# A transformer block on one core: the products of weights and values from f16 halves in three passes

## What is computed

```python
qkv = jnp.einsum('bsh,oh->bso', x, w_qkv)
q, k, v = jnp.split(qkv, [H * D, (H + HKV) * D], axis=-1)
...
scores = jnp.einsum('bhqd,bhkd->bhqk', q, k) / jnp.sqrt(jnp.float32(D))
causal = jnp.triu(jnp.ones((s, s), dtype=bool), k=1)
scores = jnp.where(causal, -jnp.inf, scores)
weights = jax.nn.softmax(scores, axis=-1)
attn = jnp.einsum('bhqk,bhkd->bhqd', weights, v)
attn = attn.transpose(0, 2, 1, 3).reshape(b, s, H * D)
return jnp.einsum('bsd,od->bso', attn, w_o)
```

## Time and profile before

| | us |
|---|---|
| median of 3 runs | 1461.82 |
| lowest and highest | 1461.27, 1463.99 |
| the profiled execution, its own time | 1461.52 |
| its span | 1459.7 |
| TensorE busy | 1370.3 (94%) |
| VectorE busy | 861.9 (59%) |
| ScalarE busy | 649.9 (45%) |
| GpSimd busy | 393.5 (27%) |

### The profile page before, as it was taken

How to read it: one execution, slowest core, us unless ns; L and a number is a source line. 1 busy time by engine, 2 the same in 40 slices (tenths; PEclk the granted TensorE clock), 3 DMA queues, 4 the chain that set the end, 5 groups by cost and what they waited for, 6 DMA issues and landing times.

```text
span 1459.7 us, 31431 instructions
## 1 busy us (share of the span) xinstructions
PE 1370.3 (94%) x11264; PEld 876.5 (60%) x11264; DVE 861.9 (59%) x2052; ACT 649.9 (45%) x1447; POOL 393.5 (27%) x311
## 2 busy tenths in 40 slices
PE   2699999999999999799999999999999679999997
PEld 1466666666666666556666666666666445555554
DVE  8877777777777777734454444545445587444433
ACT  2433333333333333436666666666666312232322
POOL 6644444444444444211112111111211283000000
PEclk9799999999999999899999999999999899999999
DMA  8300000000000000311111112111111440000000
GB/s 276 118 1 0 0 0 0 0 0 0 0 0 0 0 0 0 128 59 49 43 42 42 42 42 70 56 42 42 42 42 30 196 145 1 24 1 22 0 24 23
DMA packets 22271, 58.34 MB, mean 40 GB/s; under 512 B 1262, under 2 KB 9454, under 8 KB 19026
## 3 DMA queue, kind: packets, MB, share of 16 engines
q1 hardware_dynamic: 22226, 57.74, 12.0%
HBM read 54.46 MB, written 3.28 MB: 40 GB/s over the span
## 4 chain that ended last, share of the span: by engine, by line
PE 88%; DVE 6%; POOL 2%; issue 2%; ACT 1%; DMA 1%; DVEq 0%; SPq 0%; POOLq 0%; ACTq 0%
PE A L1386 20%; PE A L1302 16%; PE A L1354 11%; PE C L1607 10%; PE C L1410 6%; PE B L1427 5%; PE C L1340 3%; PE C L1321 3%; PE A L1622 3%; PE B L1622 3%; PE B L1395 2%; PE B L1313 2%; PE B L1333 1%; PE B L1434 1%; POOL qk L476 1%
## 5 line engine op out<-in xcount | busy, mean ns | idle before, releaser
L1302 PE MATMUL A<-arena,xh 128*100 128x512 f16 x768 | 184.1, 383 | 22.6 <-DVE arena L1054 14.4
L1386 PE MATMUL A<-wxh,arena 128*122 128x512 f16 x768 | 198.4, 381 | 0.0
L1607 PE MATMUL C<-arena 128*128 128x400 f16 x1024 | 188.4, 338 | 8.7 <-DVE arena L982 8.7
L424 POOL TENSOR_TENSOR arena<-arena,region 100x512 f32<-100x512 f32 (+1 forms) x64 | 65.9, 1062 | 427.0 <-DVE region L943 427.0
L401 POOL TENSOR_TENSOR region<-tb,ub 100x512 f32<-100x512 f32 x80 | 108.5, 1356 | 265.1 <-DVE ub L830 265.1
L1354 PE MATMUL A<-arena,stageb 128*100 128x512 f16 x768 | 175.8, 379 | 0.7 <-ACT arena L569 0.7
L1607 PEld LDWEIGHTS C<-arena 128*128 128x128 bf16 x1024 | 101.8, 99 | 85.5 <-issue 15.4
L1302 PEld LDWEIGHTS A<-arena,xh 128*100 128x100 f16 x768 | 94.7, 126 | 93.1 <-issue 20.9
L522 ACT ACTIVATE region<-C,negm 100x100 f32<-100x100 f32 x256 | 84.2, 347 | 145.9 <-DVE negm L869 145.9
L585 ACT ACTIVATE arena<-C 122x1600 f32<-122x1600 f32 x96 | 144.4, 1504 | 4.6 <-PE C L1410 2.5
L1354 PEld LDWEIGHTS A<-arena,stageb 128*100 128x100 f16 x768 | 94.0, 125 | 62.7 <-ACT arena L569 1.1
(11 more groups left out here) (174 smaller groups left out, 2318.3 us busy)
## 6 DMA issues: line engine op xcount, KB each, us to landing
stageb<-in_wffn SPq DMA_DIRECT2D x16, 768.0 KB, 4.7
arena<-in_ctxt SPq DMA_DIRECT2D x16, 722.0 KB, 4.6
stageb<-in_wffn SPq DMA_DIRECT2D x8, 1024.0 KB, 4.8
arena<-in_wqkv SPq DMA_DIRECT2D x4, 1024.0 KB, 13.8
arena<-in_wffn SPq DMA_DIRECT2D x4, 1024.0 KB, 5.8
out_x<-xres SPq DMA_DIRECT2D x16, 200.0 KB
arena<-in_wx SPq DMA_DIRECT2D x3, 1024.0 KB, 8.2
xres<-in_x SPq DMA_DIRECT2D x1, 3000.0 KB
```

Source lines behind the costliest of these rows:

```text
L424: pool.tensor_tensor(t, t, r, ALU.mult).then_inc(sig["g_kn"], 1)
L1302: ins = pe.matmul(A[j % 2][0:S, :], xp[:, k, :], wp[:, j, k, :], start=(n == 0), stop=(n == 11))
L1386: ins = pe.matmul(A[(par + n) % 2][0:rows, :], lhs, wp[:, 0 if n == 0 else 1 if n < 4 else 2, k, :], start=(i == 0), stop=(i == 11))
L1607: ins = pe.matmul(C[2 * (e % 2) + half][:, 0:UB * S], wf[:, 3 * (e // 4) + half, k, (e % 4) * 128:(e % 4 + 1) * 128], part[:, k, :], start ...
```

## The change

The turned weights and the values are each kept as two f16 halves (ph and pl, vh and vl, scaled by SP = 256 and SV = 32), and `attend` sums three f16 products, vh x ph, vh x pl and vl x ph, in place of one with fp32 operands. ScalarE makes the high halves in the copies that it made before. VectorE makes the low halves with five new instructions a batch: `p_lo` for each group, `v_lo` once. TensorE's waits for a_pT and a_v become waits for d_plo and d_vlo. The factor 1 / (SP SV) goes into a_hi and a_lo. Where one wait of TensorE implies another, the other is left out.

```diff
-        pT = carve([S, H * S])
+        ph = carve([S, H * S], F16)
+        pl = carve([S, H * S], F16)
...
-        vv = sb("vv", [S, HKV * D])
+        vh = sb("vh", [S, HKV * D], F16)
+        vl = sb("vl", [S, HKV * D], F16)
...
             def v_of(b):
...
-                act.activation(vv[:], A[1][0:S, :], ACT.Copy, scale=1.0 / (SX * SW)).then_inc(sig["a_v"], 1)
+                act.activation(vh[:], A[1][0:S, :], ACT.Copy, scale=SV / (SX * SW)).then_inc(sig["a_v"], 1)
...
             def p_back(b, g):
                 wait(act, "pe_pT", b, g + 1)
                 wait(act, "pe_av", b - 1, g + 1)
-                act.activation(pT[:, g * 400:(g + 1) * 400], B[g % 2][0:S, 0:400], ACT.Copy)\
+                act.activation(ph[:, g * 400:(g + 1) * 400], B[g % 2][0:S, 0:400], ACT.Copy, scale=SP)\
                    .then_inc(sig["a_pT"], 1)
...
+            def p_lo(b, g):
+                wait(dve, "a_pT", b, g + 1)
+                wait(dve, "pe_av", b - 1, g + 1)
+                dve.scalar_tensor_tensor(pl[:, g * 400:(g + 1) * 400], B[g % 2][0:S, 0:400], SP,
+                                         ph[:, g * 400:(g + 1) * 400], ALU.mult, ALU.subtract)\
+                   .then_inc(sig["d_plo"], 1)
+
+            def v_lo(b):
+                wait(dve, "a_v", b, 1)
+                wait(dve, "pe_av", b - 1, 4)
+                dve.scalar_tensor_tensor(vl[:], A[1][0:S, :], SV / (SX * SW), vh[:], ALU.mult, ALU.subtract)\
+                   .then_inc(sig["d_vlo"], 1)
...
             proj(0, 4)
             dve.wait_ge(ld_x, 16)
+            v_lo(0)
             row_stats(1, ssq[:, 20:21])
...
                 row_stats(0 if last else b + 2, ssq[:, 20:21])
+                p_lo(b, 0)
+                p_lo(b, 1)
                 proj(b + 1, 4)
+                p_lo(b, 2)
+                p_lo(b, 3)
                 a_lo(b, 0)
                 head_norm(b + 1)
...
                 for g in range(1, 4):
                     a_lo(b, g)
+                v_lo(b + 1)
                 for g in range(4):
                     z_back(b + 1, g)
...
             wait(dve, "pe_zT", b, 5)
+            for g in range(2):
+                p_lo(b, g)
 
             st.chain(dve.memset(xssq, 1.0))
             row_stats2(1)
-            for n in range(3):
+            square_sums(0, 0)
+            for g in range(2, 4):
+                p_lo(b, g)
+            for n in range(1, 3):
                 square_sums(0, n)
...
             def x_turn(b):
 
                 wait(pe, "d_xn", b, 1)
-                wait(pe, "a_v", b - 1, 1)
+                wait(pe, "d_vlo", b - 1, 1)
...
             def project(b, j):
                 if j == 0:
-                    wait(pe, "a_xhi", b, 1)
                     wait(pe, "d_xlo", b, 1)
                     wait(pe, "d_x1", b - 2, 1)
                 elif j >= 2:
-                    wait(pe, "a_sq", b, j - 1)
-                    wait(pe, "d_t", b, j - 1)
+
                     wait(pe, "d_u", b, j - 1)
...
             def z_turn(b, g):
                 wait(pe, "g_z", b, g + 1)
                 if g < 2:
-                    wait(pe, "a_pT", b - 1, 3 + g)
+                    wait(pe, "d_plo", b - 1, 3 + g)
...
             def p_turn(b, g):
...
                 elif g >= 2:
-                    wait(pe, "a_pT", b, g - 1)
+                    wait(pe, "d_plo", b, g - 1)
...
             def attend(b, g):
-                wait(pe, "a_pT", b, g + 1)
+                wait(pe, "d_plo", b, g + 1)
                 if g == 0:
-                    wait(pe, "a_v", b, 1)
-                pe.matmul(C[g][:, 0:400], vv[:, g * D:(g + 1) * D], pT[:, g * 400:(g + 1) * 400],
-                          start=True, stop=True).then_inc(sig["pe_av"], 1)
+                    wait(pe, "d_vlo", b, 1)
+                n = 0
+                for v, pt in ((vh, ph), (vh, pl), (vl, ph)):
+                    ins = pe.matmul(C[g][:, 0:400], v[:, g * D:(g + 1) * D], pt[:, g * 400:(g + 1) * 400],
+                                    start=(n == 0), stop=(n == 2))
+                    n += 1
+                ins.then_inc(sig["pe_av"], 1)
...
             def scores2(b, u):
-                t = (2 * u + 1) // NC
-                wait(pe, "a_T", b, t + 1)
-                wait(pe, "d_T", b, t + 1)
+                if u == 0:
+                    wait(pe, "a_T", b, 1)
+                    wait(pe, "d_T", b, 1)
```

More of the change, by code:

```diff
@@ L35 @@
 SH = 8.0
+SP = 256.0
+SV = 32.0
 VW = 2 * XD
@@ L255, in build @@
                    d_xn=1, d_zT=5, d_xlo=1, d_negm=4, d_t=5, d_u=5, d_ssq=5, d_rstd=1, d_rinv=4,
-                   d_alo=4, d_x1=1, g_w=5, g_z=5, g_p=4,
+                   d_alo=4, d_x1=1, d_plo=4, d_vlo=1, g_w=5, g_z=5, g_p=4,
                    pe_xT2=1, pe_proj=7, pe_T=4, pe_sc=6, pe_pv=4, pe_oT=2,
@@ L535, in a_hi @@
                 act.activation(ah[:, 4 * g:4 * g + 4, :], C[g][:, 0:400].rearrange("p (h s) -> p h s", h=4),
-                               ACT.Copy, scale=SA).then_inc(sig["a_ahi"], 1)
+                               ACT.Copy, scale=SA / (SP * SV)).then_inc(sig["a_ahi"], 1)
             def ctx_hi(b):
@@ L880, in a_lo @@
                 dve.scalar_tensor_tensor(al[:, 4 * g:4 * g + 4, :],
-                                         C[g][:, 0:400].rearrange("p (h s) -> p h s", h=4), SA,
+                                         C[g][:, 0:400].rearrange("p (h s) -> p h s", h=4), SA / (SP * SV),
                                          ah[:, 4 * g:4 * g + 4, :], ALU.mult, ALU.subtract)\
                    .then_inc(sig["d_alo"], 1)
+            def p_lo(b, g):
[9 more added lines that the diff above has]
+                   .then_inc(sig["d_vlo"], 1)
             def add_attn(b):
@@ L1366, in project2 @@
                 if n == 0:
-                    wait(pe, "a_x2", b, 1)
                     wait(pe, "d_x2", b, 1)
@@ L1370, in project2 @@
                 elif n == 1:
-                    wait(pe, "a_ctx", b, 1)
                     wait(pe, "d_ctx", b, 1)
@@ L1512, in _ @@
             project_out(b)
-            wait(pe, "a_pT", b, 4)
+            wait(pe, "d_plo", b, 4)
             turn_heads(0, 0, 0)
@@ L1568, in turn @@
                 if end < 1:
-                    wait(pe, "a_x2", b + 2, 1)
                     wait(pe, "d_x2", b + 2, 1)
@@ L1582, in turn @@
                 if end < 2:
-                    wait(pe, "a_T", b + 1, 1)
-                    wait(pe, "d_T", b + 1, 1)
                     turn_heads(b + 1, 1, odd)
```

## The result

The changed kernel takes 1490.92 us (median; 1490.14 to 1497.78) against 1462.36: ratio 1.0205, 95% interval 1.0173 to 1.0237. It is 2% slower, by 28.6 us; 34.1 were forecast, on the side and by the mechanism forecast. The profiled execution took 1490.14 us with a span of 1488.3, 28.6 more than before. The run of 1497.78 had a mean granted clock of 0.978 where the others had 0.980 to 0.982; what differed in it isn't known, since only the one execution has a trace.

What follows compares the result with a forecast made beforehand. TensorE was taken to bound the self attention (busy 529.57 of 530.90 us). Fifteen turns +29.9, last batch +2.3 and start +1.9 gave +34.1 on 1461.52: 1495.6 us, range 1484 to 1506.

Steps and rivals of the forecast that it cites:

- The first stall: In a middle self-attention turn, TensorE's first product of weights and values waits for p_lo(0): 1.77 us.
- steps 1 and 2: p_lo(0) runs 299.54 to 300.11; the first product follows 0.15 us after, at 300.26 instead of 298.49.
- The second stall: In a middle self-attention turn, TensorE's third product waits for p_lo(2): 1.13 us.
- step 5: Third product of a middle turn starts at 303.09, a stall of 1.13 us; the fourth at 303.60, done at 304.11.
- the gain of the passes: Four products on TensorE take 2.04 us with three f16 passes each instead of 2.94: 0.90 us a batch.
- The upper end: Range end of 1506 us: p_lo at 0.61 adds 7.5 us, two register instructions before each p_lo another 3.
- The end of the group follows p_lo(3) one for one: In each turn, the end of the four products is set by p_lo(3), VectorE's last low half.
- The last batch: Self attention's final batch, with another order on VectorE: third product stalls 2.5 us, products end 2.3 us later.
- The start: v_lo(0) in front of row_stats(1) waits for ScalarE's value copy and delays the path by 1.9 us.
- The waits left out: Dropping TensorE's implied waits gains nothing; other end 7.2 us, from the gaps before scores2 in the cross attention.
- All hidden: Rival, 4%: VectorE reaches p_lo(0) early enough, both stalls go and only the passes count: 1449 us.
- 7% to a case: Rival, 7%: new idle pieces of 1.8 and 1.1 us in self attention bring TensorE's clock down: 1536 us.

Runs made afterwards that it cites:

- row_stats late: The changed kernel with row_stats of the batch after next moved from before the first p_lo to behind the last one: 1498.76 us, ratio 1.0255.
- the passes alone: The changed kernel without low halves (no p_lo, no v_lo), all three passes taking the high halves, TensorE waiting for ScalarE's copies again: 1452.89 us, ratio 0.9947.
- cover alone: The changed kernel with only project(b+1, 5) split, eight passes before the first product and four before the third: 1474.0 us, ratio 1.0086.
- cover and order: The changed kernel with project(b+1, 5) split and a_lo(1), z_turn, x_turn and v_lo(0) also moved: 1450.51 us, ratio 0.9924.

## Why the prediction was right, point by point

- **The first stall** (steps 1 and 2: 1.77 us) measured 1.54 in 13 of the 15 turns. VectorE started p_lo(0) 1.25 us after the turn of tile 1 began, where proj(4) had started 1.40 after it, and TensorE followed within 0.06 us and not 0.15.
- **The second stall** (step 5: 1.13) measured 1.10, **the gain of the passes** (0.90) 0.86: 2.94 less 4 x 0.52. Sum: 1.54 + 1.10 - 0.86 = 1.78 against 1.75 from the starts. The turn was forecast at +1.99, measured 1.74 to 1.75 by either reading; 15 turns are 26.1 us, not 29.9. Right mechanism, a size 14% too large, nearly all in the first stall. The upper end had 3 us for the register instructions ahead of p_lo; two p_lo start 0.49 us apart, the pace of 0.48 that was forecast without them.
- **"The end of the group follows p_lo(3) one for one"**: shown by the fourth product's start 0.09 us after it, by p_lo done twice (0.61 us for each, as long as the clock held), and by row_stats late (0.34 us earlier for 0.37).
- **The last batch** (+2.3) is the term that was mis-sized most for its size: from the first turn of tiles to the end of the products 651.98 - 644.01 = 7.97 us, before 624.17 - 616.79 = 7.38, so +0.6. I had the stretch from memset to the first square sum at its old 5.25 us; it took 3.53 (646.18 to 649.71). The changed kernel, and below it two rows of the kernel before:

```profile
646.18 0.17 DVE L1158 MEMSET region<- 122x128 f32 x1
...
647.11 0.17 DVE L918 COPY statc<-stats 100x6 f32<-100x6 f32 x1
...
649.71 0.69 DVE L939 TENSOR_REDUCE region<-region 100x32 f32<-100x512 f32 x1
```

```profile
614.44 1.33 DVE L901 COPY statc<-stats 100x6 f32<-100x6 f32 x1
...
616.46 0.71 DVE L785 SCALAR_TENSOR_TENSOR nwt<-rs 100x1 f32<-100x1 f32 x1
```

  The copy of six columns had taken 1.33 us at 614.44 in the kernel before, beside GpSimd's scaling of the weights (612.47 to 615.75), and the op at 616.46 took 0.71, beside GpSimd's copy behind that (615.70 to 617.16). Each ended within 0.02 us of GpSimd. Now GpSimd was done at 645.71 and they took 0.17 and 0.16: 1.16 + 0.55 of the 1.72 us. The Trainium skill's page "SBUF — State Buffer", section "Who interferes with whom", says that certain VectorE ops and GpSimd hold a shared port pair by turns, one blocked while the other has it. Both traces fit that, and so does the run with row_stats late: in each turn before and in the changed kernel the same copy starts beside a GpSimd instruction and ends 0.03 us after it (0.41 us long, 1.09 in the first turn); with row_stats moved to where GpSimd is idle it takes 0.17 in all 15. No run moved the copy alone. By that reading about 0.25 us of the first stall (an estimate, 0.42 - 0.17) is the copy waiting for GpSimd. A duration read beside another engine's work was taken along to a place without it.
- **The start** (+1.9): 1.84.
- **The waits left out** (0, at most 7.2): the changed kernel is as fast with them; the gap before scores2 is not theirs, and 0.4 us in the cross attention is all that both pairs show.
- **The sum**: 1.84 + 26.1 + 0.6 = 28.5 us of the 28.6 between the two spans. (The start was 0.66 us later for its transfers. 1.3 us came back at the transition, where the clock rose sooner after the same idle time of 7.70 us, and 0.9 went in the cross attention, with the clock at 0.53 for 3.6 us at 678. These cancel here, by luck.)
- **The rivals.** "All hidden" did not happen, and the run of the passes alone shows that its price of 14.4 us was too high without the new order: with no VectorE at all in the way it is 9.5. The clock did not fall in the profiled execution of this kernel, but it was near: an edit that moved the holes by a few tenths of a us brought it down, and so did one that doubled p_lo. I gave 7% to a case whose trigger lay closer than the one row at 42.44 could tell. That row was also a poor witness, since the clock was low before its idle time and full behind it; the start 4 us later is the one that shows a full clock kept over idle time (timeline of TensorE, kernel before):

```profile
39.50 1.77 PE L1302 MATMUL A<-arena,xl 128*100 128x512 f16 x4
42.44 1.90 PE L1302 MATMUL A<-arena,xh 128*100 128x512 f16 x8 [1.17 <-DVE ub L830]
...
46.49 1.90 PE L1302 MATMUL A<-arena,xh 128*100 128x512 f16 x8 [1.29 <-DVE ub L830]
```

## What to carry to other kernels

When a cheaper operand form adds a step on another engine in front of a matmul, look up what that engine is doing at that moment, not its share of the stage: VectorE was free 29% of the time here and still 1.1 to 2.1 us late in each of 16 batches. The loss is the lateness of the last added step less the gain, and the cure is independent work of the bound engine placed in front of each wait, with the steps behind moved too: cover alone left +0.9%, cover and order gave -0.8%. And a faster matmul meets the next releaser soon: of 0.9 us only 0.44 came out when nothing else was moved.

## What the runs showed of the hardware

The granted clock of TensorE fell to its lower level after holes of 0.17, 0.65 and 1.47 us in a group of products (10 turns of 15), and after 2.14, 0.23 and 1.99 us (every turn), but not after 1.54 and 1.10 us (the changed kernel, none of 15 turns, its first with 2.09 and 1.10) or a single hole of 1.29 us between projections (46.49, above). The eight passes behind took 2.45 to 3.41 us instead of 1.89. A few tenths of a us in where idle time lies turned a gain of 0.3 us a turn into a kernel 8 us slower.

VectorE's copy of 100x6 elements took 0.17 us alone, and 0.21 to 1.33 beside GpSimd instructions, with whose end it ended.
